# First attention rebuilt in two parts: projections through HBM, softmax weights turned by DMA and VectorE

## What is computed

```python
h = layernorm(x)                                   # 4 x 256 x 512
kv_in = concat([ctx, h], axis=1)                   # 1601 + 256 = 1857 keys
q = (h @ Wq)      # 32 heads x 128
k = (kv_in @ Wk)  # 4 key heads x 128, each shared by 8 query heads
v = (kv_in @ Wv)
scores = einsum('bqhgd,bkhd->bhgqk', q, k) / sqrt(128)
attn = softmax(scores)
out = einsum('bhgqk,bkhd->bqhgd', attn, v).reshape(b, 256, 4096) @ Wo
x = x + out
```

## Time and profile before

| | |
|---|---|
| median of 3 runs | 3679.07 us (3677.96 to 3680.37) |
| span of the profiled execution | 3666.3 us |
| median less that span | 12.8 us |
| first attention, from the start to the last addition into x | 2662.7 us of the span |
| one batch of 32 units in the steady part | 655 us |

### The profile page before, as it was taken

The page is one execution under the profiler, slowest core; times in us unless marked ns, Lnnn a source line. Parts: engine busy times, 40 slices in busy tenths (PEclk is TensorE's granted clock), DMA queues, the critical chain, the costliest instruction groups (busy, mean ns, idle before and its releaser), DMA issues. The chain is left out here.

```text
span 3666.3 us, 65750 instructions
## 1 busy us (share of the span) xinstructions
PE 3489.8 (95%) x21978; PEld 3095.7 (84%) x21978; DVE 2331.8 (64%) x3793; ACT 1724.7 (47%) x3391; POOL 814.9 (22%) x683
## 2 busy tenths in 40 slices
PE   7999999899999999999999999999988899989999
PEld 5989889798989878898988889898867888767887
DVE  4756667575766666675666667575755666665555
ACT  4545545454544545454545545454543554542222
POOL 2312222221322222222222222231200333310000
PEclk9999999999999999999999999999989899999999
DMA  2101101210100120010102011010220111101111
GB/s 88 35 23 34 33 27 32 61 29 24 40 23 29 35 63 27 30 34 23 34 24 69 22 37 32 23 34 23 62 78 34 30 36 36 34 31 44 50 43 40
DMA packets 145533, 138.13 MB, mean 38 GB/s; under 512 B 8565, under 2 KB 102293, under 8 KB 145390
## 3 DMA queue, kind: packets, MB, share of 16 engines
q1 hardware_dynamic: 145390, 136.29, 12.3%
HBM read 134.16 MB, written 2.10 MB: 37 GB/s over the span
## 5 line engine op out<-in xcount | busy, mean ns | idle before, releaser
L552 ACT ACTIVATE a_pt_hi<-a_ps_t 128x512 fp32r<-128x512 f32 (+1 forms) x1024 | 569.3, 569 | 764.9 <-PE a_ps_t L344 757.1
L687 DVE TENSOR_TENSOR a_pt_lo<-a_ps_t,a_pt_hi 128x512 fp32r<-128x512 f32 (+1 forms) x1024 | 658.7, 654 | 275.1 <-ACT a_pt_hi L552 274.5
L694 DVE TENSOR_REDUCE a_half_max<-a_ps_s 128x1 f32<-128x1024 f32 (+1 forms) x512 | 561.8, 1121 | 176.0 <-PE a_ps_s L303 176.0
L344 PE MATMUL a_ps_t<-ident,a_probs 128*128 128x128 f32 (+1 forms) x3840 | 566.2, 272 | 22.2 <-DVE a_v_lo L771 22.2
L301 PE MATMUL a_ps_o<-a_pt_hi,a_v_hi 128*128 128x256 f32 (+1 forms) x1920 | 575.6, 300 | 11.6 <-DVE a_pt_lo L687 10.9
L559 ACT ACTIVATE a_probs<-a_ps_s,a_neg_max 128x1024 f32<-128x1024 f32 (+1 forms) x512 | 529.4, 1035 | 101.8 <-DVE a_neg_max L698 101.8
L303 PE MATMUL a_ps_o<-a_pt_hi,a_v_lo 128*128 128x256 f32 (+1 forms) x1920 | 540.7, 282 | 0.0
L302 PE MATMUL a_ps_o<-a_pt_lo,a_v_hi 128*128 128x256 f32 (+1 forms) x1920 | 539.8, 281 | 0.0
L246 POOL TENSOR_TENSOR a_wo_hi<-a_wo_raw,ones 128x512 fp32r<-128x512 f32 x128 | 133.2, 1040 | 1674.4 <-PE a_ps_m L303 1668.2
L344 PEld LDWEIGHTS a_ps_t<-ident,a_probs 128*128 128x128 f32 (+1 forms) x3840 | 449.5, 140 | 42.7 <-issue 26.0
L301 PEld LDWEIGHTS a_ps_o<-a_pt_hi,a_v_hi 128*128 128x128 f32 (+1 forms) x1920 | 362.3, 189 | 44.2 <-DVE a_pt_lo L687 31.2
(11 more groups left out here) (312 smaller groups left out, 6958.2 us busy)
## 6 DMA issues: line engine op xcount, KB each, us to landing
a_wq_raw<-in_L_xattn_Wq SPq DMA_DIRECT2D x129, 256.0 KB, 2.8
a_wo_raw<-in_L_xattn_Wo SPq DMA_DIRECT2D x128, 256.0 KB, 2.6
a_stage<-in_ctx SPq DMA_DIRECT2D x60, 256.0 KB, 2.7
c_raw<-in_ctx SPq DMA_DIRECT2D x52, 256.0 KB, 2.7
d_up_raw<-in_L_ffn_w_gate_up SPq DMA_DIRECT2D x16, 512.0 KB, 3.6
b_w_raw<-in_L_ffn_w SPq DMA_DIRECT2D x6, 1024.0 KB, 6.6
a_wkv_raw<-in_L_xattn_Wk SPq DMA_DIRECT2D x17, 256.0 KB, 3.4
a_wkv_raw<-in_L_xattn_Wv SPq DMA_DIRECT2D x17, 256.0 KB, 3.8
```

The costliest lines, as they stand in the source:

```text
L344: tr = pe.transpose(ps_t[0:n, p % 2, at:at + P], probs[a][j][:, k * P:k * P + n], ident[:, :])
L552: act.activation(pt_hi[0:n, p % 2, 0:full, :], ps_t[0:n, p % 2, 0:full * TOK].rearrange("p (k q) -> p k q", k=full), ACT.Copy).then_inc(pt ...
L687: dve.tensor_tensor(pt_lo[0:n, p % 2, 0:full, :], ps_t[0:n, p % 2, 0:full * TOK].rearrange("p (k q) -> p k q", k=full), pt_hi[0:n, p % 2, ...
L694: dve.reduce_max(half_max[:, half:half + 1], s_flat[:, lo:hi], AX.X).then_inc(max_done, 1)
```

## The change

`split_projections` is new and runs first, for all batches at once. It makes every key, value and query of the program and stores them, as pairs of high and low parts, in HBM tensors `k_all`, `v_all`, `q_all`; Wo is split and stored in `wo_all`. Its work is cut into jobs of 12 matmuls: 72 key jobs (18 chunks of tokens: for each batch three of 384 and one of 449, and two of 512 for the normalised x; times 4 key heads), 60 value jobs (one for each tile of 128 tokens, all four key heads together, tokens as the stationary operand, so that no value is transposed), and 64 query jobs (32 heads by two chunks of 512). 60 tiles of tokens are transposed on PE. ACT and DVE take each job out of PSUM as high and low part, SP stores it.

The second part loops over the 128 units. Keys and values of a group are loaded from HBM into one of two buffers during the group before, a piece in each unit; the queries and Wo of a head are loaded for each unit. The softmax weights are no longer transposed on PE. `trade` (SP) moves them inside SBUF in 4 DMAs: number c takes keys 480c to 480c + 479 of all 128 query rows and both query tiles, and puts them into partitions 32c to 32c + 31, four source partitions beside each other. The destination is one of two buffers, `xn` for even and `traded` for odd units. `turn` (DVE) then transposes blocks of 32 x 32, 512 elements in a partition at a time for a pair of key blocks, 8 times in a unit, into a ring of 4 slots. `high` (ACT) and `low` (POOL) make the two parts, SBUF to SBUF. The row sums' inverses are no longer applied at the end: they are spread over the columns (2 transposes on PE, a copy on ACT) and `scale` (DVE) multiplies the unit's output by them, so that PE sums all 32 heads of a batch in PSUM (`output` with `first_of_batch`), and DVE adds to x once for each batch. Unit u's scores and exponentials are in step u, its trade follows, its values are weighed in step u + 2, its output in step u + 3.

Core of the diff (the second part; of `split_projections` only the PE jobs):

```diff
+            def keys(q, g):
+                n, a, m = FIRST_JOB[q] + g, q % 2, even(CHUNKS[q][2])
...
+                twelve(ps_j[:, n % BANKS, 0:m], lambda c: w_hi[:, c, HD * g:HD * (g + 1)], lambda c: w_lo[:, c, HD * g:HD * (g + 1)],
+                       lambda c: hid_hi[:, a, c, 0:m], lambda c: hid_lo[:, a, c, 0:m]).then_inc(job_ps, 1)
+
+            def values(q, t):
...
+                twelve(ps_j[0:rows, n % BANKS, :], lambda c: hid_hi[:, a, c, c0:c0 + rows], lambda c: hid_lo[:, a, c, c0:c0 + rows],
+                       lambda c: w_hi[:, DC + c, :], lambda c: w_lo[:, DC + c, :]).then_inc(job_ps, 1)
...
+            def trade(u, half):
+                if not u.live:
+                    return
+                wait(sp, probs_done, 4 * u.n + 2 + half + 1)
+                if half == 0:
+                    wait(sp, turn_done, PAIRS * (u.n - 1))
+                for c in (2 * half, 2 * half + 1):
+                    n = RUN_KEYS[c]
+                    sp.dma_start(traded[u.a][SQ * c:SQ * (c + 1), :, :, 0:n], probs[:, u.a, :, RUN * c:RUN * c + n]
+                                 ).then_inc(trade_done[half], 16)
...
+            def step(b, r):
+                v = Unit(b, r - 8)
+                queries(Unit(b, r - 6))
+                trade(v, 0)
+                trade(v, 1)
+                output_weights(Unit(b, r - 9))
+                piece(Unit(b, r))
...
+            def low(u, lo, hi):
...
+                        pool.tensor_tensor(pt_lo[:, slot, 0:m, :], turned[:, slot, 0:m, :], pt_hi[:, slot, 0:m, :].bitcast(F32),
+                                           ALU.subtract).then_inc(pt_done, 1)
...
             def step(u, a, out, ahead, first_pv=False):
-                transpose_probs(v, 1 - a, 0, first_pv)
-                transpose_probs(v, 1 - a, 1, first_pv)
-                scores(u, a, 0, False)
...
+            def step(b, r):
+                u, v, w, l = Unit(b, r), Unit(b, r - 1), Unit(b, r - 2), Unit(b, r - 3)
+                scores(u, 0, 0)
+                scores(u, 0, 1)
+                weigh_values(w, 0, 4)
+                scores(u, 1, 0)
+                weigh_values(w, 4, 5)
+                scores(u, 1, 1)
+                weigh_values(w, 5, 6)
+                spread_inverses(v)
+                weigh_values(w, 6, 7)
+                output(l)
+                weigh_values(w, 7, PAIRS)
...
+            def high(u, lo, hi):
...
+                    act.wait_ge(turn_done, PAIRS * u.n + p + 1)
+                    wait(act, pv_ps, PAIRS * u.n + p + 1 - RING)
+                    act.activation(pt_hi[:, slot, 0:m, :], turned[:, slot, 0:m, :], ACT.Copy).then_inc(pt_hi_done, 1)
...
+                high(w, 2, 3)
+                widen_inverses(w)
+                high(w, 3, 4)
+                output_high(l)
+                high(w, 4, 5)
+                exponentials(u, 0, 0)
+                high(w, 5, 6)
+                exponentials(u, 0, 1)
+                high(w, 6, PAIRS)
+                high(v, 0, 2)
+                exponentials(u, 1, 0)
+                exponentials(u, 1, 1)
...
+            def turn(u, lo, hi):
...
+                    if p == 0:
+                        for half in range(2):
+                            dve.wait_ge(trade_done[half], TRADE * (u.n + 1))
+                    wait(dve, pt_done, PAIRS * u.n + p + 1 - RING)
+                    dve.transpose(turned[:, slot, 0:m, :].rearrange("p k (q r) -> p k q r", r=SQ),
+                                  traded[u.a][:, :, :, 2 * SQ * p:2 * SQ * p + SQ * m].rearrange("p g j (k r) -> p k (g j) r", k=m)
+                                  ).then_inc(turn_done, 1)
...
+                scale(l)
+                turn(w, 5, 6)
+                maximum(u, 0, 0)
+                add_output(e)
+                maximum(u, 0, 1)
+                negate_maximum(u, 0)
+                sums(v)
+                turn(w, 6, 7)
+                inverse_sums(v)
+                turn(w, 7, PAIRS)
+                tile_stats(e)
+                turn(v, 0, 1)
+                maximum(u, 1, 0)
+                turn(v, 1, 2)
+                maximum(u, 1, 1)
+                negate_maximum(u, 1)
+                turn(v, 2, 5)
```

More of the change, by code:

```diff
@@ L198, in _, with run @@
+        def run(engine, step, steps):
+            for r in range(HEADS):
+                step(0, r)
+            with engine.Fori(1, B) as b:
+                for r in range(HEADS):
+                    step(b, r)
+            for r in range(steps):
+                step(B, r)
         @block.sync
         def _(sp):
-            def load_wq(u, head):
-                sp.wait_ge(wq_ready, PRIMED + u)
-                sp.dma_start(wq_raw[:, :, :], wq_v[:, :, bass.ds(head * HD, HD)]).then_inc(wq_loaded, 16)
@@ L297, in _ @@
         @block.tensor
         def _(pe):
-            def three(out, w_hi, w_lo, m_hi, m_lo, first, last):
-                pe.matmul(out, w_hi, m_hi, start=first, stop=False)
-                pe.matmul(out, w_hi, m_lo, start=False, stop=False)
-                return pe.matmul(out, w_lo, m_hi, start=False, stop=last)
-            def project(out, w_hi, w_lo, c0, n, lo=0, hi=DC):
-                for c in range(lo, hi):
-                    mm = three(out, w_hi[:, c, :], w_lo[:, c, :], hid_hi[:, c, c0:c0 + n], hid_lo[:, c, c0:c0 + n],
-                               c == 0, c == DC - 1)
-                return mm
@@ new lines, in scores @@
+            def scores(u, j, half):
+                if not u.live:
+                    return
+                if j == 0 and half == 0:
+                    pe.wait_ge(q_loaded[u.a], 16 * (u.use + 1))
+                    if u.first_of_group:
+                        pe.wait_ge(k_loaded[u.group_a], 16 * KPIECES * (u.group_use + 1))
+                wait(pe, probs_done, 4 * u.n + 2 * j + half - 1)
+                k = k_buf[u.group_a]
+                for c in (2 * half, 2 * half + 1):
+                    c0, n = CHUNKS[c]
+                    mm = three(ps_s[:, c, 0:n], q_buf[:, u.a, 0, P * j:P * j + P], q_buf[:, u.a, 1, P * j:P * j + P],
+                               k[:, c0:c0 + n], k[:, WIDTH + c0:WIDTH + c0 + n], True, True)
+                mm.then_inc(s_ps, 1)
@@ new lines, in spread_inverses, with output @@
+            def spread_inverses(u):
+                if not u.live:
+                    return
+                pe.wait_ge(inv_done, u.n + 1)
+                wait(pe, wide_done, u.n)
+                for j in range(QT):
+                    tr = pe.transpose(ps_i[:, j * P:(j + 1) * P], row_inv[:, j:j + 1].to_broadcast([P, P]), ident[:, :])
+                tr.then_inc(inv_ps, 1)
+            def output(u):
+                if not u.live:
+                    return
+                pe.wait_ge(o_done, u.n + 1)
+                pe.wait_ge(wo_loaded[u.a], 16 * (u.use + 1))
+                if u.first_of_batch:
+                    wait(pe, y_added, QT * u.batch)
+                for j in range(QT):
+                    mm = three(ps_y[:, j, :], o_hi[:, P * j:P * j + P], o_lo[:, P * j:P * j + P], wo_buf[:, u.a, 0, :],
+                               wo_buf[:, u.a, 1, :], u.first_of_batch, u.head == HEADS - 1)
+                mm.then_inc(y_ps, 1)
```

1161 lines of the change are left out of this document (574 added, 587 removed).

## The result

The changed kernel takes **4570.6 us** (median of 4 runs, 4567.9 to 4573.2) against 3678.5 us before: 1.242 times the time, 95% interval 1.2405 to 1.2441. The forecast was 3624 us, range 3190 to 3850. The profiled execution has a span of 4571.5 us, 905 more than before.

A forecast was written before the change was run, and what follows sets the result against it. PE bound the kernel before; afterwards a chain of 15.8 us a unit. Part one 560, switch 4, ends 37, 127 periods 2007: attention 2608, 55 less; span 3611, launch 12.8: 3624 us, range 3190 to 3850.

The forecast's parts named there:

- The chain: Part two: each unit's first turn waits for the previous unit's trades; C plus D give a period of 15.8 us.
- C: Part two, from trade done to the next trade's start: turns, maxima, negation, exponential and handoffs, 5.0 us a unit.
- the 537 us of matmuls: Part one on PE: keys 142 and 22, values 166, queries 177, transposes 30; 537 us in all.
- the 14 us for waits: Part one: 14 us added for waits on stores and the barrier, so that it ends at 560 us.
- D: Part two, the four trades of a unit, 1.90 MB: 1.5 us fixed plus 9.3 at 205 GB/s, 10.8 us.
- its slow end: Trades' transfer: the rate goes with the partitions written, a quarter of 410, 102 GB/s, 18.5 us.
- the 12.8 us taken for the launch: Whole kernel: the median time stands 12.8 us above the profiled span, added to the span of 3611.
- The slower rival: Wait of the first turn: trade or turn dearer; transfer at 151 GB/s gives period 19.1, 4043 us; chance 28%.
- the turn's bound: DVE's turn at its upper bound of 1.37 us adds 1.4 to C: period 17.2, time 3802 us.
- The first rival: Trades run at other large DMAs' 302 to 410 GB/s; period 12.4 to 12.8, 3192 to 3243 us; chance 22%.
- The rule of the Trainium skill: Trades: partitions 0 to 31 reach only 8 of 16 ports; 189 GB/s, period 16.6, some 3720 us.
- The clock: PE in part two, busy 78%: costed at nothing; at most the first 2.5 us of scores double, covered by the trades.

The follow-up runs named there:

- the straight copy: Against the changed kernel, each of the four trades writes all 128 partitions, piece by piece into the same partition, in place of 32; 3192.3 us.

## Why the prediction was wrong

**What held.** The chain was the right one, and so were nearly all of its parts. C was forecast at 5.0 and is 4.86; the turn of 512 elements, taken as 0.687 from another pass, has a mean of 0.69 (658 ns over all forms, an eighth of them half as long). The four issues take 3.4 us. The first score was to start at 564 us and starts at 542.9; PE is busy all of the 270 us from 100 to 370, so the 537 us of matmuls were right and the 14 us for waits were not needed. From the first score to the first trades and from the last trades to the end of the attention it takes 15.2 and 38.1 us, 53 in place of 37, of which 8 are the longer D once more. DVE idles before the turns as forecast, PE before the scores, and the loads hide in C, as the run without them shows.

**The step that failed** is the transfer in "D, the four trades": "I take half, 205 GB/s, the geometric middle: 9.3 us. So D = 10.8". The runs show 112 GB/s, 16.9 us and D 18.45, close to what the step called its slow end, a quarter of the rate, 102 GB/s, 18.5 us. The sum closes on this one term: 127 x (18.45 - 10.8) = +972, C 127 x (4.86 - 5.0) = -18, the start of the scores -21, fill and drain +16, and +10 because the mean distance between trades over all units is 23.39 and not the 23.31 of the medians: +959, and the span is 4571.5 where 3611 was forecast.

A small term was misread beside it: the 12.8 us taken for the launch. In the executions where both are on record the time is 1.7 us above the span of the same execution (4573.21 and 4571.5 for the change; 3680.19 and 3678.5 for the kernel before). The profiled execution of before, with a span of 3666.3, must then have been some 11 us shorter than the timed ones. The median of the change stands 0.9 us under its profiled span, so the time is 947 over.

**The rivals.** The slower rival named this place and mechanism, but priced its transfer at 151 GB/s, 4043 us, and the turn's bound beside it; the slow end of the bounds, which had been worked out, entered no case and no range. That is a second fault: 18.5 us of transfer would have given a period of 25.0 and 4790 us, and the range of the forecast should have reached there. The first rival was right in its pace: once the copy is straight, the kernel takes 3192 us, the low end that was worked out for it, with PE at 98%.

**The rule of the Trainium skill** ("SBUF — State Buffer", "Door 1: The DMA port swizzle") gave 189 GB/s and some 3720 us. The Trainium skill has this rate for a DMA of 1 MiB as a whole; the prediction used it for the transfer alone, beside 1.5 us fixed. The trace agrees with that for the source in HBM: 181 GB/s, 3756 us. The Trainium skill also says there that 64 partitions reach no more ports than 32, and the runs agree (D 19.1 and 18.45). It does not give the change's own 112 GB/s: with the weights on chip as the source, the rate falls below what either side shows alone. The Trainium skill's "DMA: Bandwidth & Descriptors", section "Where 436 GB/s comes from", has on-chip copies bound at 435 GB/s; the straight copy, with slices of 339 to 410 GB/s, is not far from it, the trade is at a quarter. Even so the Trainium skill's rule was nearer than the middle between two guesses, and it spoke against the change.

**The clock.** It was costed at nothing, and a clock under 0.95 was named as a fault that was not priced. It was 0.79 in part two, with PE busy 62%, idle 9 us in each period, and its busy time 271 us longer than in the straight copy (3307.6 and 3036.6). The 0.79 is a mean of two levels. Three stretches of one period, with PE's busy time, the granted clock, DMA share and GB/s:

```profile
2000.00:2001.00 1.00, 0.00 (x0) 1.00 1.19 135
...
2003.00:2004.00 1.00, 0.00 (x0) 0.50 1.01 284
...
2012.00:2013.00 1.00, 1.00 (x6) 0.50 1.08 108
```

PE stops at 1999.1; from about 2003 to 2013 us the clock is 0.50 (1.2 GHz), and PE, which starts again at 2007.7, does its first 5.3 us of work at it. That is the doubling of the first 2.5 us of scores for which the prediction had allowed at most. In this kernel it still costs nothing on the path: C is 4.86 us at 0.79 as at 1.00, and PE has done its work by 2022.5, before the next first turn at 2025.99, so what the clock costs lies inside D, beside the trades.

**What stays open** is why a copy from 128 to 32 or 64 partitions is slower than from HBM into 32 or from 32 into 128. The number of partitions written, the odd addresses, the number of pieces and the other loads are excluded as the whole cause, and so is reading and writing the same few partitions (170 GB/s). One rival is untested: in the straight copy every row stays on its partition, in the change most rows move to another, and no run on chip moved rows from 128 partitions to 128 others. So that it is the few written partitions, and not the move together with a source of 128, is not shown. The two copies from 32 partitions, one that moves rows and one that doesn't, are near each other (158 and 170 GB/s), which speaks against the move alone.

## What to carry over

Price a DMA by its pair of ends, not by its bytes: the same 1.90 MB took 6 us of transfer from 128 partitions to the same 128 and 17 into 32 of them, and nothing in a profile of plain loads shows it. Where such a transfer stands in a chain with the work that feeds it, first take it out of the chain (here 605 us of 4571), and ask whether two fast legs over HBM with one unit more of lead beat one slow leg. And when a bound has been worked out, let the range reach it.

## What was not expected of the hardware

- The rates of the table above: 108 to 112 GB/s from 128 partitions into 64 or 32, against 319 and more into 128 and a store to HBM from the same source as fast.
- The busy share of the DMA engines is not their need: 0.93 at 137 GB/s in the change, 1.05 at 165 with the trades out of the chain, 1.01 at 343 over HBM.
- A second queue made it slower (4720 for 4571 us) until the loads behind it were gone (4360).
- SP's time to issue the four trades was not constant: 3.4 us in the change, 6.0 and 7.3 for those that read 32 partitions, and 2.6 both for those that read HBM and for those with half of each piece.
- The granted clock was at 0.50 for about 10 us of each 23, with PE idle for some 9.
